# Loads of x in the projection: issued by ACT on its own queue, instead of by SP behind the stack's writes

## What is computed

```python
def reference(x, L0_tok_weight, L0_tok_weighted_sum, ...):
    h = _L0_tok_ref(x, L0_tok_weight, L0_tok_weighted_sum)   # einsum('bhid,oi,od->bho'), x is (32, 512, 256, 4)
    h = h + _L0_attn_ref(_layernorm(h, axis=-1), ...)        # 16 heads, with relative position terms c2p and p2c
    h = h + _L0_ffn_ref(_layernorm(h, axis=-1), ...)         # 8 experts, each takes its top 512 of 16384 tokens
    return h
```

## Time and profile before

| | before |
|---|---|
| median of 3 runs | 5480.46 us (5474.0 to 5484.76) |
| profiled execution: its time, its span | 5485.72 us, 5484.0 us |
| busy in the span: PE, PEld, DVE, ACT, POOL | 86%, 61%, 64%, 48%, 29% |
| mean granted TensorE clock | 0.923 |
| transfers on the hardware queue | 1528.50 MB, 80.3% of 16 engines' span |
| `project` | up to about 1100 us, 20% of the span |

### The profile page before, as it was taken

One profiled execution on the slowest core, in us unless ns is written; L12 is line 12 of the kernel. 1 busy time (PEld: TensorE's weight loads), 2 busy tenths in 40 slices (PEclk: granted clock), 3 DMA queues, 4 the chain that ended last, 5 costly groups with the idle time before them and its releaser, 6 DMA issues. The chain is left out here.

```text
span 5484.0 us, 114121 instructions
## 1 busy us (share of the span) xinstructions
PE 4700.0 (86%) x31271; PEld 3327.9 (61%) x31272; DVE 3501.2 (64%) x9058; ACT 2614.8 (48%) x4937; POOL 1568.0 (29%) x3442
## 2 busy tenths in 40 slices
PE   6888888839899999989998998999999997773588
PEld 4666666526666666666666666666666665662555
DVE  3333333348777777777777777777777776775511
ACT  1222223226666666666666666666666663110011
POOL 1222222213323323233332323232322332550022
PEclk8999999969999999999999999999999998885599
DMA  4666666689999999999999999999999995772033
GB/s 138 222 219 218 227 219 219 203 256 363 343 343 356 350 343 347 355 351 339 348 353 341 349 354 349 339 354 345 347 352 351 350 357 198 254 253 92 4 82 78
DMA packets 661617, 1543.63 MB, mean 281 GB/s; under 512 B 39235, under 2 KB 279795, under 8 KB 661107
## 3 DMA queue, kind: packets, MB, share of 16 engines
q1 hardware_dynamic: 654966, 1528.50, 80.3%
q0 software_dynamic: 6144, 8.52, 0.9%
HBM read 762.99 MB, written 773.87 MB: 280 GB/s over the span
## 5 line engine op out<-in xcount | busy, mean ns | idle before, releaser
L998 DVE CUSTOM_DVE_ANT_1 a_scored<-a_ps_m_s,a_bias 128x512 f32<-128x512 f32 x2048 | 1397.1, 682 | 740.2 <-PE a_ps_m_s L866 739.4
L935 ACT ACTIVATE a_probsT<-a_ps_m_t 128x512 f32<-128x512 f32 x2048 | 1230.0, 607 | 1157.3 <-PE a_ps_m_t L875 1156.5
L814 POOL TENSOR_SCALAR_AFFINE_SELECT a_bias<-a_bias 128x128 f32<-128x128 f32 (+2 forms) x2560 | 921.9, 388 | 2364.8 <-DMA a_bias<-d_skew 2283.8
L875 PE MATMUL a_ps_m_t<-a_ident,a_scored 128*128 128x128 f32 x8192 | 1269.0, 278 | 0.5 <-ACT a_probsT L935 0.5
L875 PEld LDWEIGHTS a_ps_m_t<-a_ident,a_scored 128*128 128x128 f32 x8192 | 941.1, 142 | 457.4 <-DVE a_scored L1005 354.7
L929 ACT ACTIVATE a_skew_in<-a_ps_m_tab 128x512 f32<-128x512 f32 x2048 | 1124.9, 615 | 117.4 <-PE a_ps_m_tab L846 63.8
L1005 DVE TENSOR_SCALAR a_scored<-a_scored,a_top_of 128x512 f32<-128x512 f32 x2048 | 1003.2, 510 | 0.0
L866 PE MATMUL a_ps_m_s<-a_ident,a_bias 128*128 128x128 f32 x5120 | 907.3, 275 | 0.0
L861 PE MATMUL a_ps_m_s<-a_stack 99*128 99x512 bf16 (+2 forms) x2048 | 703.0, 343 | 206.0 <-issue 159.7
L846 PE MATMUL a_ps_m_tab<-a_tabs,a_stack 96*128 96x256 bf16 (+1 forms) x4096 | 716.3, 278 | 124.3 <-DMA a_stack<-d_kterm 56.1
L866 PEld LDWEIGHTS a_ps_m_s<-a_ident,a_bias 128*128 128x128 f32 x5120 | 681.7, 142 | 110.3 <-issue 7.5
(11 more groups left out here) (182 smaller groups left out, 3833.0 us busy)
## 6 DMA issues: line engine op xcount, KB each, us to landing
d_skew<-a_skew_in SPq DMA_DIRECT2D x512, 1024.0 KB, 8.4
a_bias<-d_skew SPq DMA_DIRECT2D x512, 896.0 KB, 8.9
a_stack<-d_stack SPq DMA_DIRECT2D x256, 480.0 KB
d_stack<-p_part_k SPq DMA_DIRECT2D x384, 192.0 KB
p_xt<-in_xT SPq DMA_DIRECT2D x32, 2048.0 KB, 9.6
d_stack<-p_part_q SPq DMA_DIRECT2D x384, 128.0 KB
d_ctx<-a_ctx_sb SPq DMA_DIRECT2D x128, 256.0 KB, 8.9
d_v<-p_v_sb SPq DMA_DIRECT2D x32, 544.0 KB, 4.6
```

What stands on the lines that cost most here:

```text
L814: nc.gpsimd.affine_select(blocks(r + out[0], (out[1], count)), blocks(r + of, (2, count)), pattern=[[0, count], [-sign, P]], base=0, chann ...
L875: mm = pe.transpose(m_t[:, k % 2, t * P:(t + 1) * P], scored[:, hh % SCORED, t, k * P:(k + 1) * P], ident[:])
L935: nc.scalar.activation(turned_at(hh // GH, hh % GH, k), m_t[:, k % 2], ACT.Exp, scale=SCALE).then_inc(turned, 1)
L998: nc.vector.tensor_tensor_reduce(split(scored[:, hh % SCORED, t]), split(m_s[:, t % 2]), extra, 1.0, -3.0e38, ALU.add, ALU.max, top_of[:, ...
```

## The change

The load of x leaves SP's program. ACT issues it instead, from two places in each pair of batches: x[2i+2] at the start of the pair's body, which is behind `keep_terms(2i-1)`, and x[2i+3] in batch 2i, behind the second half of `keep_h(2i+1)` and ahead of `keep_terms(2i)`. By then ACT itself has waited for the mixing that last read that half of `xt`, so no wait is added. The 30 loads, their size and their buffers stay as they were.

```diff
             def body(i, last):
                 for u in range(2):
                     n = 2 * i + u
-                    if not last:
-                        settled(sp, h_done, 2 * (n + 1), passed)
-                        sp.dma_start(xt[:, u], xT[n + 2].rearrange("d (c p) s -> p (d c) s", p=P)
-                                     ).then_inc(x_in[u], 16)
                     settled(sp, h_kept, 2 * (n + 1), passed)
...
+            def load_x(n, u):
+
+                act.dma_start(xt[:, u], xT[n].rearrange("d (c p) s -> p (d c) s", p=P)).then_inc(x_in[u], 16)
+
-            def batch(n, i, u, more):
+            def batch(n, i, u, more, load):
                 keep_turned(n)
...
                 if more:
                     keep_h(n + 1, i + u, 1 - u, 1)
+                if load:
+                    load_x(n + 3, 1 - u)
                 keep_terms(n)
...
             def body(i, last):
-                batch(2 * i, i, 0, True)
-                batch(2 * i + 1, i, 1, not last)
+                if not last:
+                    load_x(2 * i + 2, 0)
+                batch(2 * i, i, 0, True, not last)
+                batch(2 * i + 1, i, 1, not last, False)
```

## The result

The changed kernel takes 5458.89 us (median of 13 runs, 5450.89 to 5467.32), the kernel before 5477.23 us (median of 13 in all, 5463.96 to 5490.21). The ratio is 0.9965, with a 95% interval of 0.9957 to 0.9973. So it is faster, clear of the noise, but by 18 us only, about a quarter of the 70 us that were forecast. It lies outside the range.

What follows compares the result with a forecast made beforehand. PE's waits for x were taken to bound `project`; without them a loop of 29.6 us plus 0.4 us contention rules, so 29 batches x (32.43 - 30.0) = 70 us are gained, giving 5410 us, range 5365 to 5450.

Steps and rivals of the forecast that it cites:

- The bound of the kernel before: In `project`, PE's 19 waits for x, 92.8 us, with the clock falling behind them; removing them gains at most 123 us.
- The sum: Over 29 batches of `project`, 32.43 us falls to 30.0 us each, gaining 70 us, for 5410 us.
- What is late next: In `project`, the loop from SP's stack writes through key terms, ACT, POOL and DVE bounds a batch: 29.35 us.
- The size of the loop without contention: In `project`, the loop through SP takes 29.6 us a batch in the mean, before any added contention.
- the rival in which PE's own work bounds: In `project`, key terms land sooner or issues are not stretched; a batch takes 28.19 us, 5357 us in all; chance 0.13.
- The contention: In `project`, loads delay key term landings by 0.8 us a pair, 0.4 us a batch; upper end 5.5 us.
- Issuing on ACT at nothing: In `project`, ACT issuing 30 loads at 0.42 us, 12.6 us, adds nothing; 7.5 us if its cover were gone.
- contention eats half: In `project`, key terms land 2 to 5.5 us later in every pair; 5435 to 5470 us; chance 0.14.

## Why the prediction was wrong

- **The bound of the kernel before: right.** Waits for x in every second batch, with the fall of the clock behind them. They are gone, all of them. The kernel with two buffers alone confirms that they bound by themselves. The sum took each of 29 batches at 32.43 us; the last of them took 38.72, so 6 us more were there to win than it counted.
- **What is late next: right.** The loop through SP, the landing of the key terms, ACT, POOL and DVE took over. That PE would feel it as a wait for a turned copy ahead of q is what the waits show. But it was forecast to rule in every batch, and it rules only in those with a load ahead of the key terms; the others take PE's own 28.2 us. The alternation that was to go is still there.
- **The size of the loop without contention: near, partly by luck.** It was put at 29.6 us a batch. The kernel with the load behind the key terms has 30.01 us, and 5405 us in all. Two terms missed and made up for each other: its landing is 5.6 us and not 3.8, its issuing leg 19.9 us and not 20.9 to 21.4. The prediction let the leg vary and held the landing at 3.79 us, and that was wrong already in the kernel before. The key term transfer issued at 411.19, behind the shortest leg of 19.59 us, has this landing:

```profile
DMA to landing us min/median/max: 5.7/5.7/5.7
```

  With it the loop of the shortest leg is 19.59 + 0.54 + 5.7 + 4.11 = 29.9 us and not 28.0, so the rival in which PE's own work bounds stood on a number that does not hold.
- **The contention: wrong, and this is the step that failed.** "I take 0.8 us in a pair, near the low end, because the engines had 0.47 to spare", with 5.5 us as the upper end. Measured: 10.61 - 3.79 = 6.8 us in the batch shown, 2.9 to 7.3 us over the 14 batches and 9.2 - 3.8 = 5.4 us in the mean. So the upper end was about the mean, and the choice of the low end was the fault. The share of 0.53 is a mean over the stack's writes alone; with the load in flight the share is 1.03, there is nothing to spare, and in the batch of this row the key terms, issued at 535.70 and 536.24, are in it:

```profile
538.00:543.00 5.00, 4.12 (x24) 3.67 (x24) 4.00 (x8) 0.03 (x1) 0.00 (x0) 1.00 1.03 363
```

  Not all of it is the load's. With the load kept behind the key terms they still take 5.6 us. So of the 5.4 us that were added 1.8 come without a load beside the key terms, and 3.6 only with it.
- **What the late landing costs: not priced.** A wait of 6.43 us also brings the clock down. It costs 5.89 - 3.60 = 2.3 us of q on top. The prediction knew this of the wait for x and left it out of the sum and the rivals. In the mean a pair takes 64.2 us, where 60.0 was forecast: twice PE's 28.19 us, 5.1 us of wait for the copy, and 2.6 us, most of it q at the lower clock. Over the 28 batches it is 32.09 us against 30.0, and 28 x 2.09 = 59 us of the gain do not come. The last batch gives back some of this, and the median misses by 49 us.
- **Issuing on ACT at nothing: right.** 0.38 us each, and beside an activation rather than behind it (below). The kernel with the load behind the key terms issues as many and is the faster by 60 us.
- **The rival "contention eats half"** had the mechanism, its landing 2 to 5.5 us late, and gave 5435 to 5470 us. It had 0.14. The result is in it.

The Trainium skill ("DMA: Bandwidth & Descriptors", "Queues, rings and completion order") has the engines take turns between queue rows by packets, and the prediction named it beside its low end. The trace does not bear out the conclusion drawn from it, that a small transfer would not sit out a load. The load issued at 595.36 us has this landing, so it landed at 608.5 us:

```profile
DMA to landing us min/median/max: 13.1/13.1/13.1
```

The key terms, issued 2.1 us behind it, landed at 608.1 us. Over the 14 batches they landed between 3.6 us before and 1.2 us after the load, so they sat out most of it or all of it. The load was slowed as well: the 14 of these batches land in 11.4 to 13.1 us, the other loads that ACT issues in 8.3 to 10.2. That smaller rows of the load helped by 25 us would fit turns by packet. Turns alone did not give the low price. That the key terms stood in their own queue behind stack writes that had been slowed too would explain it, and was not tried.

## What to carry to other kernels

A load that is issued earlier lands in the middle of someone else's traffic: look for the small transfer whose landing somebody waits for, and price its delay with the load's whole time on the engines (here 5.5 us; 5.4 were added in the mean, 7.3 at most), however free the engines look without the load. The program point counts more than the queue; one step further down, behind the wait for that small transfer, the same load was worth 80 us instead of 18. Where a chain of landing, copy and reuse becomes the next bound, a second buffer of 3 KB a partition takes the landing out of it, and only together with the early load: alone it gave nothing. And in a chain of issuing and landing the two legs are not independent: in the kernel before, behind the fastest issues the last transfer took longest to land.

## What was not expected of the hardware

- Two loads of 2 MB in flight at once on two queues slow each other. ACT's at 502.21 us landed after 12.8 us, and PE got SP's 13.9 us after its issue, where a load of the kernel before lands in 9.6 us. Both are there 18.2 us after the first was issued, which is less than twice 9.6 us, but the one that is awaited comes later. Both halves of this change, each by itself, made the kernel slower, by 0.4% and 1.0%, and together they made it faster.
- A transfer is issued on ACT while an activation runs. The load at 534.47 us stands inside the one at 534.32 us:

```profile
534.32 0.60 ACT L464 ACTIVATE p_h_sb<-p_ps_m_h 128x512 f32<-128x512 f32 x1 [1.38 <-PE p_ps_m_h L391]
534.47 0.39 ACTq L501 DMA_DIRECT2D p_xt<-in_xT  x1
```

- With a load kept away from them, the key terms still took 5.2 to 6.5 us to land in nearly all batches, instead of 3.8. The write of h that SP issues 0.7 to 1.1 us behind them is not enough to explain it: it follows at that distance in the changed kernel too, where the key terms without a load ahead land in 3.0 to 3.9 us. What the kernel before shows is an exchange: behind its six issuing legs of 19.6 to 19.8 us the key terms landed in 4.0 to 5.7 us, behind its four longest, 22.6 us and more, in 3.1 to 4.6 us. Why is open.
